# Third stage of a decoder layer in another order: each tile's factor in its own turn, low-rank products one tile sooner, the last tile's bias first

## The chip, the core and the metric

The kernel runs on one core of one Trainium2 chip. A core has five engines that run their own instruction queues side by side and wait for one another through semaphores: TensorE (PE, matmul), VectorE (DVE), ScalarE (ACT), GpSimd (POOL) and SyncE (SP, which here only issues transfers). Matmuls write to PSUM, eight banks of 128 x 512 float32; the rest lies in SBUF. The metric is the device time in microseconds. A profile is one execution with the hardware profiler on.

## The reference, cut to what matters

One decoder layer over 32 sequences of 64 tokens (2048 tokens of 512 numbers): an attention over a gathered cache, a cross attention, and a feed-forward part, each added to `x` and followed by a layer norm. Only the third part is touched:

```
z = jnp.einsum('bsd,od->bso', x, W) + b
u = jnp.einsum('bsd,edr->ebsr', x, A)
m = jnp.einsum('ebsr,ero,e->bso', u, B, p_scores)
norm_z = jnp.linalg.norm(z, axis=-1, keepdims=True)
norm_m = jnp.linalg.norm(m, axis=-1, keepdims=True)
gamma = jnp.minimum(0.5 * norm_z / (norm_m + 1e-6), 1.0)
x = _layernorm(x + z + gamma * m)
```

## The kernel before, in words

The tokens lie in 16 tiles of 128 (`NT = 16`). Three stages run one after the other, one for each part of the layer. Every product is made of three matmuls, high by high, high by low and low by high: each operand is kept as a rounded part (`...h`, made by ScalarE) and the rest (`...l`, made by VectorE or GpSimd).

The third stage is a loop over the tiles on each engine. There is no scheduler: the order of the instructions on each engine is the order in which the code is written, and the engines meet at named semaphores. For tile `tt`:

- TensorE first turns tile `tt + 5` (`turn_acc("x3", ...)`, four transposes into one of two banks of `big[0]`), then makes `z` (`linear`, 12 matmuls of 512 columns) and `m` (`low_rank_out`, three matmuls into one of three banks, `ps_mm`). Behind every fourth tile comes `low_rank(q)`, 12 matmuls that make `u` for the next four tiles. It waits for `yTl` of the last of these four (`tile_lo`), `low_rank_out` waits for `uTl` (`ff_lo`), and for the bank of three tiles back to be read (`ff_hi`, `("gm", tt - 3)`).
- VectorE makes `yTl` of tile `tt + 5` (`tile_low`, `x_lo`), adds the bias (`z_out`, matmul result plus `fbb` into `z`), works out the factor in four small steps (`mix`, steps 1 to 4, on one number per token, each waiting for the step before), makes `uTl` (`low_rank_lo`), and does the last layer norm: `measure` (two `bn_stats`, two `bn_aggr`, one addition) and `finish` (a reciprocal, and one normalise per tile). For the last three tiles, step 5 of `mix` adds `gam * m` itself. In tiles 0 and 1 it also does `normal3`, the layer norm of the second stage for tiles 12 to 15.
- ScalarE makes `yTh` (`tile_high`), the two norms and their roots (`norms`: two squares with sums, one root into `nz`), `gm_m` (`scaled_m`, the factor times `m`), `uTh` (`low_rank_hi`), and the root of the variance (`square_root`).
- GpSimd adds `z` to the tile (`add_z`), and `gm_m` (`add_m`) for all but the last three tiles. SyncE stores two tiles at a time, the last two singly.

Before the change the factor of a tile is worked out two tiles later, between the steps of `measure` and `finish`; `scaled_m` and `add_m` follow two tiles later as well.

Of the kernel before, what the change touches and what calls it, by code (L numbers as in the profile page):

```python
# [14 lines left out]
NT = T // 128  # L15
# [239 lines left out]
def decoder_kernel(nc, xt, x, ctxt, rope, wq_v, wk_v, wv_v, wo_v, k_cache, v_cache, block_idx,  # L255
                   wq2_v, bqk_in, wkv2_v, wo2_v, xbo, fw_v, fb, fa_v, fB, fp, out):
    with ExitStack() as top:
# [430 lines left out]
        def gpsimd_program(pool):  # L688
# [136 lines left out]
            def add_m(tt):  # L825
                gate.wait_ge(ff_hi, ("gm", tt))
                gate.wait_ge(pool_add, ("z", tt))
                pool.tensor_tensor(xa(tt), xa(tt), gm_m[:, tt % 2, :], ALU.add).then_inc(pool_add(("m", tt)), 1)

            for tt in range(NT):  # L830
                if 2 <= tt and tt - 2 < NT - 3:
                    add_m(tt - 2)
                add_z(tt)


# [1 line left out]
        def scalar_program(act):  # L837
# [87 lines left out]
            def square_root(tiles, tag):  # L925
                a, b = tiles[0], tiles[-1] + 1
                gate.wait_ge(ln, ("var", tag, tiles[-1]))
                act.activation(rstd[:, a:b], mv[:, a:b, 1], ACT.Sqrt).then_inc(root((tag, tiles[-1])), 1)
# [217 lines left out]
            def low_rank_hi(q):  # L1146
                gate.wait_ge(ff_done, ("u", q))
                if q >= 1:
                    gate.wait_ge(ff_done, ("m", 4 * q - 1))
                gate.wait_ge(in_pcol, "pcol")  # L1150
                act.activation(uTh[:, :], ps_u, ACT.Identity, scale=pcol[:, 0:1]).then_inc(ff_hi(("u", q)), 1)
# [13 lines left out]
            def scaled_m(tt):  # L1165
                gate.wait_ge(ff_lo, ("mix", tt, 4))
                if tt >= 2:
                    gate.wait_ge(pool_add, ("m", tt - 2))
                act.activation(gm_m[:, tt % 2, :], ps_mm[tt % 3], ACT.Copy, scale=gam[:, tt:tt + 1]).then_inc(
                    ff_hi(("gm", tt)), 1)  # L1170

            low_rank_hi(0)
            for tt in range(NT):
                if tt + 5 < NT:
                    tile_high("x3", tt + 5)
                if 2 <= tt and tt - 2 < NT - 3:
                    scaled_m(tt - 2)
                if tt >= 4 and tt % 2 == 0:
                    square_root([tt - 4, tt - 3], 3)
                norms(tt)  # L1180
                if tt < 2:
                    square_root([12 + 2 * tt, 13 + 2 * tt], 2)
                if tt % 4 == 3 and tt // 4 + 1 < 4:
                    low_rank_hi(tt // 4 + 1)
            square_root([NT - 4, NT - 3], 3)
            square_root([NT - 2], 3)
            square_root([NT - 1], 3)

        def bank_order():
# [44 lines left out]
        def vector_program(dve):  # L1234
# [365 lines left out]
            def low_rank_lo(q):  # L1600
                gate.wait_ge(ff_hi, ("u", q))
                dve.scalar_tensor_tensor(uTl[:, :], ps_u, pcol[:, 0:1], f(uTh[:, :]), ALU.mult,
                                         ALU.subtract).then_inc(ff_lo(("u", q)), 1)
# [47 lines left out]
            def finish(tiles, step):  # L1651
                if step == 0:
                    invert_root(tiles, 3, tiles[-1])
                else:
                    gate.wait_ge(ln, ("rstd", 3, tiles[-1]))
                    normalise_tile(tiles[step - 1], 3)

            low_rank_lo(0)
            for tt in range(NT):
                if tt + 5 < NT:  # L1660
                    tile_low("x3", tt + 5)
                for step in range(4):
                    if tt >= 2:
                        mix(tt - 2, step + 1)
                    if tt >= 4 and tt % 2 == 0:
                        measure([tt - 4, tt - 3], step)
                    if tt >= 5 and tt % 2 == 1 and step < 3:
                        finish([tt - 5, tt - 4], step)
                if tt >= 2:
                    mix(tt - 2, 5)  # L1670
                z_out(tt)
                if tt < 2:
                    normal3([12 + 2 * tt, 13 + 2 * tt])
                if tt % 4 == 3 and tt // 4 + 1 < 4:
                    low_rank_lo(tt // 4 + 1)
            for step in range(4):
                measure([NT - 4, NT - 3], step)
                mix(NT - 2, step + 1)
            mix(NT - 2, 5)
            for step in range(3):  # L1680
                mix(NT - 1, step + 1)
                measure([NT - 2], step)
                finish([NT - 4, NT - 3], step)
            mix(NT - 1, 4)
            mix(NT - 1, 5)
            measure([NT - 1], 0)
            finish([NT - 2], 0)
            measure([NT - 1], 1)
            finish([NT - 2], 1)
            measure([NT - 1], 2)  # L1690
            finish([NT - 1], 0)
            finish([NT - 1], 1)

        def tensor_program(pe):
# [410 lines left out]
            for tt in range(NT):  # L2107
                if tt + 5 < NT:
                    turn_acc("x3", tt + 5)
                linear(tt)  # L2110
                low_rank_out(tt)
                if tt % 4 == 3 and tt // 4 + 1 < 4:
                    low_rank(tt // 4 + 1)

        programs = (tensor_program, vector_program, scalar_program, gpsimd_program, sync_program)
# [68 lines left out]
```

## Time and profile before

| | us |
|---|---|
| median of 3 runs (2915.19 to 2920.72) | 2916.35 |
| profiled execution | 2922.1 |
| its span | 2920.3 |
| TensorE busy in the span | 2813.9 (96%) |
| VectorE busy | 1858.0 (64%) |
| ScalarE busy | 1505.8 (52%) |
| GpSimd busy | 1484.5 (51%) |

The page puts the third stage into the last of its 40 slices: of the span from 2834 to 2906 us TensorE is busy 68.63 of 72 us, VectorE 48.96; from 2906 to 2921 TensorE is busy 0.54 us, VectorE 11.38. Matmuls overlap in their rows (a matmul's row of 512 columns is 0.39 us long while the next starts after 0.23), so the time of a piece of TensorE's work is read from starts.

### The profile page before, as it was taken

The numbers are of one execution on the slowest core, as the hardware profiler recorded it, in microseconds if no ns is written. First come the engines' busy times: TensorE is split into PE (matmuls) and PEld (weight loads), VectorE is DVE, ScalarE is ACT, GpSimd is POOL, SyncE is SP. The second block draws the span as 40 slices with busy tenths as digits, with TensorE's granted clock in tenths as the row PEclk, the third lists the DMA queues.
The fourth block names the chain that finished last, engine by engine and source line by source line (L and its number), as shares of the span: only waits on it lengthen the run. The fifth ranks groups of instructions, "written<-read, shape, count | busy, mean of one in ns | idle before, by whom it ended". The sixth has DMA issues, their size and how long they took to land.

```text
span 2920.3 us, 68000 instructions
## 1 busy us (share of the span) xinstructions
PE 2813.9 (96%) x28800; PEld 2532.8 (87%) x28800; DVE 1858.0 (64%) x3294; ACT 1505.8 (52%) x3202; POOL 1484.5 (51%) x1256
## 2 busy tenths in 40 slices
PE   7999999999999999999999889999999999999997
PEld 6888888888888888888888889999999999999976
DVE  6677677677666666666666665655555566555566
ACT  5555655655565555656555544433344444343344
POOL 6777777776766666666666641212123312121124
PEclk8999999999999999999999999999999999999999
DMA  5323313313414321222222231111111111111101
GB/s 166 86 75 94 101 56 102 101 54 93 109 63 144 86 80 55 79 86 63 76 79 78 60 97 35 41 33 43 39 46 49 55 34 41 34 41 33 30 19 58
DMA packets 91500, 197.96 MB, mean 68 GB/s; under 512 B 20668, under 2 KB 21308, under 8 KB 89148
## 3 DMA queue, kind: packets, MB, share of 16 engines
q1 hardware_dynamic: 71480, 154.80, 18.6%
q10 hardware_dynamic: 17664, 34.61, 3.5%
q0 software_dynamic: 2048, 4.20, 0.6%
q8 instruction: 227, 3.72, 0.5%
q14 instruction: 81, 0.63, 0.1%
HBM read 176.78 MB, written 16.78 MB: 66 GB/s over the span
## 4 chain that ended last, share of the span: by engine, by line
PE 65%; DVE 19%; issue 6%; ACT 5%; POOL 2%; DMA 2%; ACTq 1%; SPq 0%; DVEq 0%; POOLq 0%
PE big L1708 28%; PE bank L1708 18%; PE bank L1800 11%; DVE nmx L1317 5%; PE big L1780 5%; DVE P L1323 4%; PE big L1800 3%; DVE xacc L1345 2%; DVE rall L1339 2%; DVE qTl L1312 2%; ACT qTh L849 1%; ACT P L894 1%; ACT pth L903 1%; DMA gathered<-in_k_cache,idx 1%; ACT oTh L909 1%
## 5 line engine op out<-in xcount | busy, mean ns | idle before, releaser
L729 POOL TENSOR_TENSOR ptl<-P,pth 128x576 fp32r<-128x576 f32 x512 | 725.1, 1435 | 180.8 <-ACT pth L903 179.9
L894 ACT ACTIVATE P<-big,nmx 128x576 f32<-128x576 f32 x512 | 379.3, 741 | 309.4 <-DVE nmx L1317 302.5
L1800 PE MATMUL bank<-pth,v 32*128 32x256 f32 x4608 | 432.4, 283 | 30.1 <-DVE xacc L1345 14.6
L1800 PE MATMUL big<-pth,v 32*128 32x256 f32 x4608 | 433.1, 283 | 6.4 <-issue 6.4
L1323 DVE STREAM_TRANSPOSE P<-P 128x576 f32<-128x576 f32 x512 | 386.8, 765 | 70.5 <-ACT P L894 68.2
L1800 PEld LDWEIGHTS bank<-pth,v 32*128 32x128 f32 x4608 | 391.0, 188 | 46.0 <-issue 42.6
L1317 DVE TENSOR_REDUCE nmx<-big 128x1 f32<-128x576 f32 x512 | 377.8, 749 | 6.3 <-PE big L1780 2.8
L1800 PEld LDWEIGHTS big<-pth,v 32*128 32x128 f32 x4608 | 368.4, 188 | 6.9 <-issue 6.7
L903 ACT ACTIVATE pth<-P 128x576 fp32r<-128x576 f32 x512 | 347.3, 681 | 49.2 <-DVE P L1323 48.8
L1800 PE MATMUL bank<-ptl,v 32*128 32x256 f32 x2304 | 358.1, 280 | 0.7 <-issue 0.7
L1800 PE MATMUL big<-ptl,v 32*128 32x256 f32 x2304 | 335.6, 280 | 0.0
L809 POOL TENSOR_TENSOR P<-P,sm 128x512 f32<-128x512 f32 x64 | 66.9, 1046 | 456.3 <-DVE sm L1543 456.3
L734 POOL TENSOR_TENSOR oTl<-rall,oTh 128x256 fp32r<-128x256 f32 x256 | 183.4, 738 | 210.1 <-ACT oTh L909 210.1
L1708 PE MATMUL big<-yTl,wqTh 128*128 128x256 f32 x1008 | 285.2, 283 | 0.0
L1708 PE MATMUL big<-yTh,wqTl 128*128 128x256 f32 x1008 | 285.2, 283 | 0.0
L1708 PE MATMUL big<-yTh,wqTh 128*128 128x256 f32 x1008 | 285.2, 283 | 0.0
L1466 DVE SCALAR_TENSOR_TENSOR xql<-big,bqk,xqh 128x256 fp32r<-128x256 f32 x252 | 110.1, 478 | 234.3 <-ACT xqh L1030 233.9
L909 ACT ACTIVATE oTh<-rall 128x256 fp32r<-128x256 f32 x256 | 93.5, 412 | 316.6 <-DVE rall L1339 316.6
L1800 PEld LDWEIGHTS bank<-ptl,v 32*128 32x128 f32 x2304 | 252.8, 188 | 1.5 <-issue 1.5
L1780 PE MATMUL big<-kTh,qTh 128*128 128x288 f32 x1024 | 232.6, 309 | 14.7 <-ACT P L894 12.6
L1030 ACT ACTIVATE xqh<-big,bqk 128x256 fp32r<-128x256 f32 x252 | 105.8, 471 | 252.6 <-PE big L1708 252.6
L1780 PEld LDWEIGHTS big<-kTh,qTh 128*128 128x128 f32 x1024 | 178.1, 190 | 66.6 <-issue 26.4
(277 smaller groups left out, 8367.5 us busy)
## 6 DMA issues: line engine op xcount, KB each, us to landing
rall<-kept_r ACTq DMA_DIRECT2D x64, 512.0 KB
raw<-in_wo SPq DMA_DIRECT2D x64, 256.0 KB, 2.8
raw<-in_wq SPq DMA_DIRECT2D x62, 256.0 KB, 2.8
v<-kept_v SPq DMA_DIRECT2D x24, 448.0 KB
v<-kept_v SPq DMA_DIRECT2D x68, 128.0 KB, 3.1
raw<-in_xWq SPq DMA_DIRECT2D x33, 256.0 KB, 2.7
raw<-in_xWo SPq DMA_DIRECT2D x32, 256.0 KB, 2.7
rawb<-in_xWo SPq DMA_DIRECT2D x32, 256.0 KB, 2.7
```

The lines of the kernel that those rows point to most:

```text
L729: pool.tensor_tensor(third_columns(ptl, i), blocks_of(i), f(third_columns(pth, i)), ALU.subtract).then_inc(p_low(i), 1)
L734: pool.tensor_tensor(out_quarter(ol[:, :, :], a), rall_quarter(a), f(out_quarter(oh[:, :, :], a)), ALU.subtract).then_inc(o_low((k, a)), 1)
L894: act.activation(P[:, i % PSLOTS, :].rearrange("p (k n) -> p k n", k=2), ps_s[i % 2][:, :, 0:HALF], ACT.Exp, bias=nmx[:, i % 8:i % 8 + 1], ...
L903: act.activation(third_columns(pth, i), blocks_of(i), ACT.Copy).then_inc(p_hi(i), 1)
L909: act.activation(out_quarter(oh[:, :, :], a), rall_quarter(a), ACT.Copy).then_inc(o_hi((k, a)), 1)
L1030: act.activation(q2h[:, :, p, 64 * j:64 * j + 64], ps[:, 256 * j:256 * j + 256].rearrange("p (b i) -> p b i", i=64), ACT.Identity, bias=bq ...
L1317: dve.tensor_reduce(nmx[:, i % 8:i % 8 + 1], ps_s[i % 2][:, :, 0:HALF], AX.XY, ALU.max, negate=True).then_inc(max_done(i), 1)
L1323: dve.transpose(P[:, i % PSLOTS, :], P[:, i % PSLOTS, :]).then_inc(p_turned(i), 1)
L1466: dve.scalar_tensor_tensor(q2l[:, :, p, 64 * j:64 * j + 64], ps[:, 256 * j:256 * j + 256].rearrange("p (b i) -> p b i", i=64), bqk[:, h:h ...
L1708: t = pe.matmul(dst, a, b, start=first and i == 0, stop=final and end)
L1780: m = pe.matmul(ps_s[i % 2][:, h, 0:HALF], l, r[:, HALF * h:HALF * h + HALF], start=j == 0, stop=j == 2)
L1800: m = pe.matmul(ps_o[a][:, 0:256], v[r, s, l, :], p[r, lo:hi + 1:hi - lo, block_of(b), :, :], start=first, stop=final)
```

## The change

It changes the order of the third stage, and nothing of what is computed.

- VectorE: in the turn of tile `tt` the order is now `tile_low(tt + 5)`, `z_out(tt)`, `low_rank_lo` where there is one, `measure` or `finish` of an older pair, and then all steps of `mix(tt)`. Before, `mix(tt - 2)` stood between the steps of `measure` or `finish`, ahead of `z_out(tt)`. The last tile's `z_out` now stands ahead of everything else in its turn.
- ScalarE and GpSimd: `scaled_m` and `add_m` are one tile behind the tile, not two; `low_rank_hi` stands ahead of the norms of its tile; the roots of the variance move with `measure`.
- TensorE: `low_rank` of the next four tiles is behind the third tile of four, not the fourth.

```diff
@@ gpsimd_program
             for tt in range(NT):
-                if 2 <= tt and tt - 2 < NT - 3:
-                    add_m(tt - 2)
+                if 1 <= tt and tt - 1 < NT - 3:
+                    add_m(tt - 1)
                 add_z(tt)
@@ scalar_program
                 if tt + 5 < NT:
                     tile_high("x3", tt + 5)
-                if 2 <= tt and tt - 2 < NT - 3:
-                    scaled_m(tt - 2)
-                if tt >= 4 and tt % 2 == 0:
-                    square_root([tt - 4, tt - 3], 3)
+                if 1 <= tt and tt - 1 < NT - 3:
+                    scaled_m(tt - 1)
+                if tt % 4 == 3 and tt // 4 + 1 < 4:
+                    low_rank_hi(tt // 4 + 1)
                 norms(tt)
                 if tt < 2:
                     square_root([12 + 2 * tt, 13 + 2 * tt], 2)
-                if tt % 4 == 3 and tt // 4 + 1 < 4:
-                    low_rank_hi(tt // 4 + 1)
-            square_root([NT - 4, NT - 3], 3)
-            square_root([NT - 2], 3)
+                if tt == NT - 2:
+                    square_root([NT - 4, NT - 3], 3)
+                elif tt == NT - 1:
+                    square_root([NT - 2], 3)
+                elif tt >= 3 and tt % 2 == 1:
+                    square_root([tt - 3, tt - 2], 3)
             square_root([NT - 1], 3)
@@ vector_program
                 if tt + 5 < NT:
                     tile_low("x3", tt + 5)
-                for step in range(4):
-                    if tt >= 2:
-                        mix(tt - 2, step + 1)
-                    if tt >= 4 and tt % 2 == 0:
-                        measure([tt - 4, tt - 3], step)
-                    if tt >= 5 and tt % 2 == 1 and step < 3:
-                        finish([tt - 5, tt - 4], step)
-                if tt >= 2:
-                    mix(tt - 2, 5)
                 z_out(tt)
+                if tt % 4 == 3 and tt // 4 + 1 < 4:
+                    low_rank_lo(tt // 4 + 1)
                 if tt < 2:
                     normal3([12 + 2 * tt, 13 + 2 * tt])
-                if tt % 4 == 3 and tt // 4 + 1 < 4:
-                    low_rank_lo(tt // 4 + 1)
...
+                if tt == NT - 1:
+                    for step in range(3):
+                        finish([NT - 6, NT - 5], step)
+                        measure([NT - 2], step)
+                elif tt == NT - 2:
+                    for step in range(4):
+                        measure([NT - 4, NT - 3], step)
+                elif tt >= 3 and tt % 2 == 1:
+                    for step in range(4):
+                        measure([tt - 3, tt - 2], step)
+                elif tt >= 4:
+                    for step in range(3):
+                        finish([tt - 4, tt - 3], step)
+                for step in range(5):
+                    mix(tt, step + 1)
             for step in range(3):
-                mix(NT - 1, step + 1)
-                measure([NT - 2], step)
+                measure([NT - 1], step)
                 finish([NT - 4, NT - 3], step)
...
+            for step in range(2):
+                finish([NT - 2], step)
+            for step in range(2):
+                finish([NT - 1], step)
@@ tensor_program
                 linear(tt)
                 low_rank_out(tt)
-                if tt % 4 == 3 and tt // 4 + 1 < 4:
+                if tt % 4 == 2 and tt // 4 + 1 < 4:
                     low_rank(tt // 4 + 1)
```

TensorE before, from the third tile's `m` (`bank<-wkvTh,uTh`) on: the turn of tile 8 (`ident,xaccb`), `z` and `m` of tile 3, and then the low-rank product (`bank<-yTh,xTh`), of which the first rows stand here; the rest of each product is left out.

```order
L1708 MATMUL bank<-wkvTh,uTh 128x512
...
L1701 MATMUL big<-ident,xaccb 128x128 [waits ln,tile_lo]
...
L1708 MATMUL big<-xTh,yTh 128x512 [waits ff_lo]
...
L1708 MATMUL big<-wkvTh,uTh 128x512 [waits ff_hi]
...
L1708 MATMUL bank<-yTh,xTh 128x512 [waits tile_lo]
```

The same place now:

```order
L1706 MATMUL bank<-wkvTh,uTh 128x512
...
L1706 MATMUL bank<-yTh,xTh 128x512 [waits tile_lo]
...
L1699 MATMUL big<-ident,xaccb 128x128 [waits ln]
...
L1706 MATMUL big<-xTh,yTh 128x512 [waits ff_lo]
...
L1706 MATMUL big<-wkvTh,uTh 128x512 [waits ff_hi]
```

The low-rank product has moved ahead of tile 3's products and of the turn of tile 8; its wait for tile 7's `yTl` (`tile_lo`) comes that much sooner.

VectorE before, in the turn of tile 1, behind its bias (`z`): the layer norm of tiles 14 and 15, then at once `yTl` of tile 7 and the factor of tile 0.

```order
L1611 TENSOR_TENSOR z<-big,fbb 128x512 [waits ff_done]
L1353 BN_STATS stat<-xaccb 128x6 x2
...
L1367 TENSOR_SCALAR xaccb<-xaccb,mv,rstd 128x512
L1239 TENSOR_TENSOR yTl<-big,yTh 128x4x128 [waits tile_hi]
L1617 TENSOR_SCALAR nz<-nz 128x1 [waits ff_hi]
```

Now:

```order
L1613 TENSOR_TENSOR z<-big,fbb 128x512 [waits ff_done]
L1355 BN_STATS stat<-xaccb 128x6 x2
...
L1369 TENSOR_SCALAR xaccb<-xaccb,mv,rstd 128x512
L1619 TENSOR_SCALAR nz<-nz 128x1 [waits ff_hi]
L1622 RECIPROCAL nz<-nz 128x1 [waits ff_lo]
L1625 SCALAR_TENSOR_TENSOR gam<-nz 128x1 [waits ff_lo]
L1628 TENSOR_SCALAR gam<-gam 128x1 [waits ff_lo]
L1241 TENSOR_TENSOR yTl<-big,yTh 128x4x128 [waits tile_hi]
```

The factor of tile 1 itself, with its wait for the norms (`ff_hi`), stands ahead of `yTl` of tile 7.

VectorE before, from the last bias on; the mixes of tiles 14 and 15 are the rows with `gam,xaccb`.

```order
L1611 TENSOR_TENSOR z<-big,fbb 128x512 [waits ff_done]
L1641 BN_STATS stat<-xaccb 128x6 [waits pool_add]
...
L1648 TENSOR_SCALAR mv<-mv 128x2 [waits ln]
L1626 TENSOR_SCALAR gam<-gam 128x1 [waits ff_lo]
L1630 SCALAR_TENSOR_TENSOR xaccb<-bank,gam,xaccb 128x512 [waits pool_add,ff_lo]
L1617 TENSOR_SCALAR nz<-nz 128x1 [waits ff_hi]
...
L1626 TENSOR_SCALAR gam<-gam 128x1 [waits ff_lo]
L1630 SCALAR_TENSOR_TENSOR xaccb<-big,gam,xaccb 128x512 [waits pool_add,ff_lo]
```

Now:

```order
L1613 TENSOR_TENSOR z<-big,fbb 128x512 [waits ff_done]
L1366 RECIPROCAL rstd<-rstd 128x2 [waits root]
L1643 BN_STATS stat<-xaccb 128x6 [waits acc_done]
L1369 TENSOR_SCALAR xaccb<-xaccb,mv,rstd 128x512 [waits ln]
L1647 BN_AGGR mv<-stat 128x2 [waits ln]
L1369 TENSOR_SCALAR xaccb<-xaccb,mv,rstd 128x512
L1650 TENSOR_SCALAR mv<-mv 128x1 [waits ln]
L1619 TENSOR_SCALAR nz<-nz 128x1 [waits ff_hi]
...
L1628 TENSOR_SCALAR gam<-gam 128x1 [waits ff_lo]
L1632 SCALAR_TENSOR_TENSOR xaccb<-big,gam,xaccb 128x512 [waits pool_add,ff_lo]
```

Tile 14's factor and mix have moved ahead of the last bias, and so have the statistics of tiles 12 and 13; two normalises of an older pair have moved in behind it.

## Rows read from the trace of the kernel before

**Rows 1.** Waits of TensorE, 2824 to 2921: total us, times, longest.

```profile
PE bank L1708 <- ACT gm_m L1169: 1.3, 1, 1.3
PE big L1708 <- ACT gm_m L1169: 0.8, 1, 0.8
PE bank L1708 <- DVE uTl L1602: 0.7, 1, 0.7
...
PE big L1708 <- DVE nz L1617: 0.5, 1, 0.5
```

**Rows 2.** Timeline of TensorE: start, length, engine, line, operation, tiles.

```profile
2841.69 0.60 PE L1701 MATMUL big<-ident,xacc 128*128 128x128 f32 x4
...
2845.56 0.60 PE L1701 MATMUL big<-ident,xaccb 128*128 128x128 f32 x4
...
2849.45 0.39 PE L1708 MATMUL bank<-yTh,xTh 128*128 128x512 f32 x1
...
2852.17 0.60 PE L1701 MATMUL big<-ident,xaccb 128*128 128x128 f32 x4
...
2892.03 0.39 PE L1708 MATMUL big<-xTh,yTh 128*128 128x512 f32 x1
...
2906.16 0.39 PE L1708 MATMUL big<-wkvTh,uTl 128*128 128x512 f32 x1
```

**Rows 3.** Timeline of all engines, 2909 to 2919.

```profile
2909.30 0.68 DVE L1611 TENSOR_TENSOR z<-big,fbb 128x512 f32<-128x512 f32 x1
...
2911.34 0.20 ACT L1163 ACTIVATE nz<-nrm 128x2 f32<-128x2 f32 x1
...
2914.62 0.75 DVE L1630 SCALAR_TENSOR_TENSOR xaccb<-big,gam,xaccb 128x512 f32<-128x512 f32 x1
...
2917.28 0.55 DVE L1367 TENSOR_SCALAR xaccb<-xaccb,mv,rstd 128x512 f32<-128x512 f32 x1
```

**Rows 4.** Timeline of VectorE in the first tiles of the stage.

```profile
2841.93 0.68 DVE L1239 TENSOR_TENSOR yTl<-big,yTh 128x512 fp32r<-128x512 f32 x1
2842.53 0.68 DVE L1611 TENSOR_TENSOR z<-big,fbb 128x512 f32<-128x512 f32 x1
2843.13 1.27 DVE L1353 BATCH_NORM_STATS2 stat<-xaccb 128x6 f32<-128x512 f32 x2
...
2844.72 0.17 DVE L1358 TENSOR_SCALAR mv<-mv 128x2 f32<-128x2 f32 x1
...
2846.28 0.68 DVE L1239 TENSOR_TENSOR yTl<-big,yTh 128x512 fp32r<-128x512 f32 x1
2846.88 0.14 DVE L1617 TENSOR_SCALAR nz<-nz 128x1 f32<-128x1 f32 x1
...
2847.53 0.69 DVE L1611 TENSOR_TENSOR z<-big,fbb 128x512 f32<-128x512 f32 x1
```

**Rows 5.** Timeline of all engines, 2887.7 to 2891.3.

```profile
2887.76 0.69 ACT L1169 ACTIVATE gm_m<-bank,gam 128x512 f32<-128x512 f32 x1 [2.39 <-DVE gam L1626]
...
2888.52 1.29 POOL L828 TENSOR_TENSOR xaccb<-xaccb,gm_m 128x512 f32<-128x512 f32 x1 [2.47 <-ACT gm_m L1169]
...
2888.77 1.33 DVE L1367 TENSOR_SCALAR xacc<-xacc,mv,rstd 128x512 f32<-128x512 f32 x1
...
2889.77 1.48 POOL L823 TENSOR_TENSOR xaccb<-xaccb,z 128x512 f32<-128x512 f32 x1
...
2890.02 1.25 DVE L1623 SCALAR_TENSOR_TENSOR gam<-nz 128x1 f32<-128x1 f32 x1
```

**Rows 6.** Transfers issued from 2895 to 2921: count, size, us to landing.

```profile
out<-xaccb SPq DMA_DIRECT2D x2, 256.0 KB, 2.0
```

**Rows 7.** Stretches: length, busy time by engine, granted clock, transfers.

```profile
1664.00:1668.00 4.00, 2.09 (x10) 1.40 (x8) 2.35 (x6) 0.91 (x2) 4.00 (x4) 1.00 0.61 146
1704.00:1708.00 4.00, 1.14 (x9) 0.93 (x10) 3.96 (x6) 1.95 (x4) 3.58 (x3) 1.00 0.24 67
1708.00:1712.00 4.00, 4.00 (x24) 4.00 (x23) 3.65 (x6) 0.60 (x1) 1.75 (x2) 0.57 0.90 283
```

More of the change, by code:

```diff
@@ L1661, in vector_program @@
                     tile_low("x3", tt + 5)
-                for step in range(4):
-                    if tt >= 2:
-                        mix(tt - 2, step + 1)
-                    if tt >= 4 and tt % 2 == 0:
-                        measure([tt - 4, tt - 3], step)
-                    if tt >= 5 and tt % 2 == 1 and step < 3:
-                        finish([tt - 5, tt - 4], step)
-                if tt >= 2:
-                    mix(tt - 2, 5)
                 z_out(tt)
+                if tt % 4 == 3 and tt // 4 + 1 < 4:
+                    low_rank_lo(tt // 4 + 1)
                 if tt < 2:
                     normal3([12 + 2 * tt, 13 + 2 * tt])
-                if tt % 4 == 3 and tt // 4 + 1 < 4:
-                    low_rank_lo(tt // 4 + 1)
[L1676 to L1679, printed above, removed]
+                if tt == NT - 1:
[13 more added lines that the diff above has]
+                    mix(tt, step + 1)
             for step in range(3):
-                mix(NT - 1, step + 1)
-                measure([NT - 2], step)
+                measure([NT - 1], step)
                 finish([NT - 4, NT - 3], step)
[L1684 to L1692, printed above, removed]
+            for step in range(2):
+                finish([NT - 2], step)
+            for step in range(2):
+                finish([NT - 1], step)
         def tensor_program(pe):
```

## The prediction

> **What bounds the kernel now.** I read four views, in this order: the page's busy table and slices (where the third stage lies), the waits of TensorE in that stage, the timeline of TensorE and of VectorE there, and the timeline of all engines behind the last matmul. Everything before about 2836 us of the span is untouched by the change, so only the last 85 us can move. The reader is to see three things.
>
> First, TensorE is the bound up to its last matmul, with four gaps: two in which a low-rank output product waits for `gm_m` (it needs the psum bank that ScalarE reads for `gm_m` three tiles back), one for `uTl`, and one put down to a small VectorE step, which is also the place of a `uTl` wait [rows 1]. As idle time they are 3.4 us. By starts it is a little more: a tile is 2845.56 - 2841.69 = 3.87 us of TensorE with its four transposes, a low-rank product 2852.17 - 2849.45 = 2.72 us, so a product of 512 columns starts every 0.227 us and a tile without transposes takes 15 x 0.227 = 3.40 us [rows 2]. From 2852.17 (tile 4 begins) to 2892.03 (tile 12 begins) stand 39.86 us for 7 x 3.87 + 3.40 + 2 x 2.72 = 35.93 us of work: 3.9 us lost. From there to the start of the last product at 2906.16 stand 14.13 us for 4 x 3.40 - 0.23 = 13.37: 0.7 us lost [rows 2].
>
> Second, VectorE is already behind at the end. The last bias addition (`z`, tile 15) starts at 2909.30, while the products it adds to were done about 2905.9 (0.46 before 2906.16, with a product's row of 0.39 behind its start) [rows 2, 3]: 3.4 us late.
>
> Third, from that bias the kernel needs 11.0 us to the end of the span at 2920.3: the norms (the root `nz` starts at +2.04), the last mix at 2914.62 (+5.3), the last normalise at 2917.28, done at 2917.83, and the store, 2.5 us [rows 3].
>
> **What the change removes.** (a) `gm_m` of a tile is asked for one tile earlier. A third bank back is two tile times, over 7 us, away from then on; both `gm_m` waits go. (b) The low-rank product of the next four tiles is issued behind the third tile of four, not the fourth, so `uTl` has a whole output product and 12 matmuls of cover: it still has to wait for the fourth tile's output product, which reads the old `uTh`, then costs about 0.7 on ScalarE and 0.7 on VectorE, and has 3.1 us until it is needed. Both `uTl` waits go. Sum removed: 3.9 before tile 12 and 0.7 behind it, -4.6 us if nothing takes their place.
>
> **What it adds: the wait of VectorE in its own turn.** The factor's four small steps now stand behind the bias of the same tile, and everything VectorE does for the next tile is queued behind them. The first step waits until ScalarE has the norms: 2.04 + 0.20 = 2.24 us behind the start of the bias [rows 3], of which the bias takes 0.60 (2843.13 - 2842.53) [rows 4]. Standing alone the four steps take 2847.53 - 2846.88 = 0.65 us, since each waits for the one before [rows 4]; between the statistics of another tile they are nearly hidden today.
>
> First place, the low-rank product of tiles 4 to 7, worked out in span times. VectorE now does the factor of tile 0 at 2841.93 (the end of the first late normalise), so `yTl` of tile 6 starts at 2842.58, the bias of tile 1 at 2843.18, the statistics and normalise of tiles 14 and 15 at 2843.78; these take 2846.28 - 2843.13 = 3.15, to 2846.93; the factor of tile 1 to 2847.58; and `yTl` of tile 7 is done at 2848.27 [rows 4]. TensorE wants it at the end of tile 2, at 2845.56 [rows 2]. It waits until about 2848.3, +2.8 us, where before it found it ready. The gap is new, and the change puts it there by moving the product past tile 3: +2.8 and 0.1 for a slower first matmul.
>
> Second and third place, the same product for tiles 8 to 11 and 12 to 15. Here the cover is VectorE's lag. In an odd tile VectorE does `yTl` 0.60, bias 0.60, two statistics with their short steps 2844.72 - 2843.13 + 0.1 = 1.69, factor 0.65: 3.5 us, under 3.87. In an even tile it does `yTl` 0.60, bias 0.60, a reciprocal 0.20, two normalises of 0.46 and the factor: 2.97 alone. But a normalise and the third step of the factor are held by GpSimd: beside GpSimd's two additions they took 1.33 and 1.25 us, where the same forms take about 0.5 and 0.15 otherwise; the first ended 0.29 after the addition of 2888.52 (2889.81), the second with the addition of 2889.77 (2891.25) [rows 5].
> The Trainium skill ("SBUF — State Buffer", Who interferes with whom) says the same of the cause: a VectorE operation in a two-port mode, or one with two SBUF inputs, shares one port pair with GpSimd, and whoever starts first holds it for the whole instruction; the trace agrees (1.33 and 1.25). By that rule the new order meets the lock in every even tile; without it the even tile would be 3.0 us and the rival "VectorE keeps up" below would be the forecast.
> In the new order `gm_m` follows the factor at once (0.69 long, GpSimd 0.76 behind its start [rows 5]), so GpSimd adds m of the tile before, then z, just when VectorE normalises. Followed through from tile 4 (bias at 2859.7, 1.2 late, because tile 3 also holds `uTl` behind its output product): factor of tile 4 done 2863.3, bias of tile 5 2863.9, factor of tile 5 2867.0, `yTl` of tile 11 2867.7. TensorE wants it at 2866.7: +1.1 us. Tiles 8 to 10 repeat tiles 4 to 6: again +1.1. Bounds for each of the two: 0 (VectorE not late) and 2.8 (as at the first place). I take 1.1, the chain followed row by row.
>
> Sum up to the start of tile 12: -3.9 + 2.9 + 1.1 + 1.1 and 0.2 to 0.3 of slower starts = +1.5 us, so 2893.5 for 2892.03. With the 0.7 behind it gone, TensorE ends about 0.8 later than before.
>
> **The end.** Tile 12 on, TensorE needs 3.40 per tile, VectorE more: factor and the held normalises in tile 12 (factor done 2901.4 to 2901.9), statistics of 10 and 11, factor held by the addition of z, and the mix (0.67) in tile 13, statistics of 12 and 13, factor and mix in tile 14. That gives the last bias at 2909.6 to 2910.1, about 3.4 us behind its products: as late as today. Putting that bias first removes what stood ahead of it in its own tile only, not the lag that comes from tile 14's order.
> Behind it: one statistics and two normalises of tiles 10 and 11 lie in the 1.6 us in which VectorE would wait for the norms, the first of them held by the addition of z, so the factor starts 0.6 after `nz`; the mix starts at +3.6 against +5.3 today. That is the gain of 1.7 us. Then the normalises of 12, 13 and 14 stand ahead of that of 15, where today only part did: done 3.94 behind the mix's start, today 3.21 (2917.83 - 2914.62): +0.7. And the stores of 12 and 13 (one transfer), of 14 and of 15 (256 KB, 2.0 us to landing each) are now issued within 1.4 us instead of 3.3 [rows 6]; the last may queue, 0 to 1, I take 0.6.
> Last bias to end: 11.0 - 1.7 + 0.7 + 0.6 = 10.6. End of span 2920.2 to 2920.7 against 2920.3: **about +0.2 us, nothing**. The profiled execution took 2922.1 us (1.8 around its span); the median of the runs is 5.75 us lower, and I take the difference over to it: 2916.35 + 0.2, or 2916.5.
>
> **Rivals.**
> *VectorE keeps up* (faster). Normalises and additions miss each other, the waits at the second and third low-rank product are 0, and VectorE reaches tile 15 hardly late. Tile 12 starts at 2892.03 - 3.9 + 2.9 = 2891.0, the products of tile 15 are done 13.1 later at 2904.1, the bias starts at about 2904.6, and 9.6 later is 2914.2: -6.1 us, 2910.2. For it: alone, the even tile takes 3.0. Against: the lock is in the rows [rows 5], and VectorE is 3.4 us late today with less waiting in its queue.
> *VectorE falls further behind* (slower). Both later low-rank products wait as long as the first: 2 x 1.7 more; and each pair of the last tiles costs an extra held operation, some 1 us a pair: +2.1. Sum 0.2 + 3.4 + 2.1 = +5.7: 2922.1. It decides from the point where a pair of tiles costs VectorE more than the 18.2 us that TensorE has for four (4 x 3.87 + 2.72), that is over 9.1. My pairs are at 8.2 and less.
> *The clock falls* in the new gap of 2.8 us. Where TensorE was busy 1.14 of 4 us the granted clock of the next 4 us was 0.57, so mostly at the lower level, 1.2 GHz; where it was busy 2.09 of 4 us it stayed at 1.00, 2.4 GHz [rows 7]. The new gap leaves 1.2 of 4, or more if it lies across two stretches, but work of 2.7 us goes on right behind it. Price: 4 us at 0.57, some 1.7 to 3.4 us more: 2919.
> The Trainium skill ("TensorE: Matmul & The Clock Gate", HAM oscillation) warns that an idle gap brings the slow level back; the row of 1708 shows it, that of 1664 shows a gap that did not.
>
> **How the numbers follow.** Forecast, no change to speak of: 0.74. VectorE keeps up: 0.12. Falls further behind: 0.07. Clock: 0.07. A measurement of this kernel tells about 0.2%, 5.8 us, from nothing. The first rival is just beyond it, a VectorE that keeps up only in part is not, and noise may push the forecast's lower edge over it: faster 0.13. Slower by the second rival and a part of the third: 0.07. Same: 0.80. The likeliest case alone lies within 2913 to 2920 (0 or 2.8 at two places, 0 to 1 at the store); with the rivals 2911 to 2921.5.
>
> **What would show it.** No `gm_m` or `uTl` wait of TensorE; one wait for `yTl` at the first moved low-rank product, some 2.8 us, and two of about 1; normalises of 1.3 us in even tiles; last bias about 2910 and 3 us behind its products; mix 3.6 behind it. I am wrong if the two later `yTl` waits are absent, if the last bias comes by 2906, or if the granted clock leaves 1.00 before the last matmul.

## The result, and the profile after

| | before | after |
|---|---|---|
| median of 14 runs each, same chip (us) | 2918.08 | 2923.48 |
| ratio after to before, 95% interval | | 1.0017 (1.0010 to 1.0025) |
| profiled execution / its span (us) | 2922.1 / 2920.3 | 2927.96 / 2926.2 |
| transposes of tile 7 to the end of the span (us) | 78.61 | 83.28 |

The change makes the kernel slower, by 5 us (2.9 to 7.3), which is 0.17%; the forecast was no change, 2911 to 2921.5 us, and the time lies outside its range. One execution in these runs, of the kernel "steps between", took 7002.51 us and is left out of its ratio. Of the 7.0 us between the forecast of 2916.5 and the 2923.48 measured, 1.7 belong to the kernel before, whose median is 2918.08 over 14 runs where the three runs at hand gave 2916.35; the rest is what the change did beyond the forecast.

The last line of the table is the measure used below. The place at which the third stage begins shifts from one execution to the next by some us (between 2835.33 and 2844.52 in the twelve traces of this study) through stages that no kernel here touches. So stretches are counted from the start of the transposes of tile 7 [rows 2], and not spans. By it the change costs +4.67 us, close to what the medians say. Each stretch is from one execution, so small differences need care: in "last bias first" below nothing differs from the kernel before until the last tile's turn on VectorE, and yet TensorE's last product comes 0.2 us later. Over all kernels below, differences of stretches and of medians agree within 1.3 us.

Waits of TensorE after, from 2824 on (engine, tile and line, what it waited for, us in total, times, longest), which answer to [rows 1]:

```profile
PE bank L1706 <- DVE yTl L1241: 7.2, 4, 3.3
PE big L1699 <- DVE yTl L1241: 1.0, 1, 1.0
```

All waits for `gm_m` and `uTl` are gone. One wait for `yTl` is there at each low-rank product; the rest of these two rows lies ahead of the stage. The timeline of TensorE (start, length, then line, operation and tiles; idle time before it in brackets), which answers to [rows 2]:

```profile
2842.92 0.60 PE L1699 MATMUL big<-ident,xacc 128*128 128x128 f32 x4
...
2850.25 0.47 PE L1706 MATMUL bank<-yTh,xTh 128*128 128x512 f32 x1 [3.30 <-DVE yTl L1241]
...
2854.67 0.60 PE L1699 MATMUL big<-ident,xaccb 128*128 128x128 f32 x4
...
2872.03 0.47 PE L1706 MATMUL bank<-yTh,xTh 128*128 128x512 f32 x1 [1.67 <-DVE yTl L1241]
...
2892.21 0.47 PE L1706 MATMUL bank<-yTh,xTh 128*128 128x512 f32 x1 [1.68 <-DVE yTl L1241]
...
2898.45 0.39 PE L1706 MATMUL big<-xTh,yTh 128*128 128x512 f32 x1
...
2911.82 0.39 PE L1706 MATMUL big<-wkvTh,uTl 128*128 128x512 f32 x1
```

The three waits are 3.46, 1.83 and 1.85 us by starts. By starts means: from the end of the 0.23 us that a product needs to the start of the next one. The first product also takes 4.42 us (2854.67 - 2850.25), where the second takes 2.85 (to 2874.88). The stretches around it (length, busy time of TensorE, weight loads, VectorE, ScalarE, GpSimd, then the granted clock) tell why:

```profile
2846.00:2850.00 4.00, 0.95 (x5) 0.45 (x3) 3.52 (x12) 1.90 (x6) 1.36 (x2) 1.00 0.00 0
2850.00:2854.00 4.00, 3.75 (x11) 2.98 (x12) 1.33 (x6) 1.73 (x6) 2.52 (x2) 0.65 0.00 0
2854.00:2858.00 4.00, 4.00 (x20) 3.21 (x19) 0.69 (x1) 1.18 (x2) 1.29 (x1) 0.92 0.00 0
```

From 2850 to 2854 the granted clock was 0.65: most of the product ran at the lower level, 1.2 GHz. Its matmuls start every 0.23 us up to 2851.29, a microsecond behind the gap, and every 0.43 us from there to 2854.28. VectorE and GpSimd at the first and the second place:

```profile
2846.07 1.29 POOL L823 TENSOR_TENSOR xacc<-xacc,z 128x512 f32<-128x512 f32 x1
...
2846.73 0.66 DVE L1360 TENSOR_SCALAR mv<-mv 128x2 f32<-128x2 f32 x1
...
2849.42 0.68 DVE L1241 TENSOR_TENSOR yTl<-big,yTh 128x512 fp32r<-128x512 f32 x1
...
2863.34 0.68 DVE L1613 TENSOR_TENSOR z<-big,fbb 128x512 f32<-128x512 f32 x1
...
2864.13 2.29 DVE L1369 TENSOR_SCALAR xacc<-xacc,mv,rstd 128x512 f32<-128x512 f32 x2
...
2867.58 0.68 DVE L1613 TENSOR_TENSOR z<-big,fbb 128x512 f32<-128x512 f32 x1
...
2869.12 1.29 POOL L823 TENSOR_TENSOR xacc<-xacc,z 128x512 f32<-128x512 f32 x1
...
2869.78 0.66 DVE L1650 TENSOR_SCALAR mv<-mv 128x2 f32<-128x2 f32 x1
...
2871.19 0.69 DVE L1241 TENSOR_TENSOR yTl<-big,yTh 128x512 fp32r<-128x512 f32 x1
```

From bias to bias VectorE needs 4.24 us in the even tile (2.29 of it two normalises beside GpSimd's additions) and then 3.61 us to `yTl` of the odd one. A small addition that took 0.17 at 2844.72 before [rows 4] took 0.66: it was held by GpSimd's addition of `z`, that is, it started at 2846.73 and ended with that addition, at 2847.4. (No wait of VectorE for a result of GpSimd is in this trace.) The end, which answers to [rows 3] and [rows 6]:

```profile
2915.37 0.68 DVE L1613 TENSOR_TENSOR z<-big,fbb 128x512 f32<-128x512 f32 x1
...
2918.94 0.75 DVE L1632 SCALAR_TENSOR_TENSOR xaccb<-big,gam,xaccb 128x512 f32<-128x512 f32 x1
...
2922.35 0.55 DVE L1369 TENSOR_SCALAR xaccb<-xaccb,mv,rstd 128x512 f32<-128x512 f32 x1
```

```profile
out<-xaccb SPq DMA_DIRECT2D x2, 256.0 KB, 2.8
```

The last bias is 3.8 us behind its products (done about 2911.53) and the mix 3.57 behind the bias; 10.83 us from the bias to the end.

### The profile page after: what moved, and what is told of

It reads as the page before. It is cut to its first block, busy times and chain, and to the rows that moved or that the text cites. A ratio compares the mean times of both kernels' runs of the same rounds, so it can differ in the third digit from the quotient of the medians.

```text
span 2926.2 us, 68008 instructions
## 1 busy us (share of the span) xinstructions
PE 2817.4 (96%) x28800; PEld 2536.0 (87%) x28800; DVE 1865.4 (64%) x3294; ACT 1505.2 (51%) x3202; POOL 1482.7 (51%) x1256
## 3 DMA queue, kind: packets, MB, share of 16 engines
q8 instruction: 227, 3.72, 0.5%
## 4 chain that ended last, share of the span: by engine, by line
PE 65%; DVE 20%; ACT 6%; issue 4%; DMA 2%; POOL 1%; ACTq 1%; SPq 0%; DVEq 0%; POOLq 0%
PE big L1706 28%; PE bank L1706 18%; PE bank L1798 11%; DVE nmx L1319 5%; PE big L1778 5%; DVE P L1325 4%; PE big L1798 3%; DVE xacc L1347 2%; DVE rall L1341 2%; DVE qTl L1314 2%; ACT qTh L849 1%; ACT P L894 1%; ACT pth L903 1%; ACT oTh L909 1%; PE bank L1699 1%
## 5 line engine op out<-in xcount | busy, mean ns | idle before, releaser
L1798 PE MATMUL bank<-pth,v 32*128 32x256 f32 x4608 | 433.2, 283 | 27.1 <-DVE xacc L1347 15.3
L1798 PEld LDWEIGHTS big<-pth,v 32*128 32x128 f32 x4608 | 368.8, 188 | 10.6 <-issue 10.4
```

The lines of the kernel that those rows point to most:

```text
L1798: m = pe.matmul(ps_o[a][:, 0:256], v[r, s, l, :], p[r, lo:hi + 1:hi - lo, block_of(b), :, :], start=first, stop=final)
```

## The experiments

"Stretch" is the time from the transposes of tile 7 to the end, in one profiled execution; "last product" is its part up to the start of TensorE's last product; "late" is from the end of the last tile's products to its bias; "end" from that bias on. A median difference is to runs of the kernel before on the same chip.

| kernel | ratio to before (95%) | stretch | last product | late | end |
|---|---|---|---|---|---|
| before | 1 | 78.61 | 64.47 | 3.4 | 11.0 |
| after | 1.0017 (1.0010 to 1.0025) | 83.28 | 68.90 | 3.8 | 10.8 |
| product back | 0.9981 (0.9973 to 0.9990) | 73.33 | 61.08 | 1.7 | 10.8 |
| late norm later | 1.0005 (0.9996 to 1.0014) | 79.78 | 65.40 | 3.8 | 10.8 |
| short additions | 0.9997 (0.9989 to 1.0006) | 77.28 | 66.06 | 1.3 | 10.2 |
| product only | 1.0004 (0.9995 to 1.0012) | 79.23 | 65.91 | 2.6 | 11.0 |
| bias first in each tile | 0.9982 (0.9973 to 0.9991) | 73.84 | 61.58 | 1.7 | 10.8 |
| before, bias first | 1.0011 (1.0002 to 1.0020) | 82.08 | 67.23 | 0 | 15.3 |
| last bias first | 1.0002 (0.9993 to 1.0011) | 79.49 | 64.68 | 0 | 15.1 |
| gap filled | 1.0009 (1.0000 to 1.0018) | 81.56 | 67.25 | 3.8 | 10.8 |
| factor sooner only | 1.0005 (0.9996 to 1.0013) | 80.67 | 66.61 | 4.3 | 10.0 |
| steps between | 0.9969 (0.9958 to 0.9980) | 72.75 | 60.86 | 1.4 | 10.7 |

### The product back

```diff
-                if tt % 4 == 2 and tt // 4 + 1 < 4:
+                if tt % 4 == 3 and tt // 4 + 1 < 4:
                     low_rank(tt // 4 + 1)
```

and `low_rank_hi` behind `norms`, `low_rank_lo` behind `mix` of that tile.

> The changed kernel with one part undone: TensorE's low-rank product for the next four tiles stands behind the fourth tile of four again (uTh behind the norms, uTl behind the factor of that tile). Theory A (the product asked for too soon): the three waits for yTl (3.46, 1.83 and 1.85 us by starts) go, with them the slow clock behind the first (1.6 us), and waits for uTl of 0.5 to 0.8 us each come back: 8.7 - 2.1 = 6.6 us less than the changed kernel, a little under the kernel before (2916 to 2917 beside 2918.1). Theory B (VectorE, waiting for the norms in its own turn, is too slow as such): the lag shows at the next place instead, a tile's yTl or the z bank, with 1 to 2 us per four tiles, and at most 3 us are won back: 2920 or more.

Ten us less than the changed kernel (73.33 for 83.28), and by the medians 5.5 less than the one before. TensorE keeps one wait of size, 1.0 for `uTl`. What sets this kernel apart from the one before is seen in VectorE's waits from 2848 to 2900; first before, then here:

```profile
DVE yTl L1239 <- ACT yTh L842: 12.5, 6, 2.1
DVE uTl L1602 <- ACT uTh L1151: 6.5, 3, 2.2
```

```profile
DVE nz L1619 <- ACT nz L1163: 1.6, 1, 1.6
DVE z L1613 <- PE big L1706: 1.5, 2, 0.8
```

Before, VectorE stood 2.09 us in each of six tiles, waiting for `yTh`, which ScalarE makes only after the norms of the tile before, and about as long for `uTh` in the three others. In the new order the older pair's statistics or normalises stand behind the bias and fill the time in which ScalarE makes the norms. So the new order on VectorE, ScalarE and GpSimd is worth 5 us, and the product one tile sooner loses 10 on top of it. Theory A holds, and gives more than the 6.6 it forecast: 7.8 up to the last product, and the last bias follows its products 2.1 us sooner than in the changed kernel.

### The second late layer norm one tile later

```diff
-                if tt < 2:
-                    normal3([12 + 2 * tt, 13 + 2 * tt])
+                if tt in (0, 2):
+                    normal3([12 + tt, 13 + tt])
```

> The changed kernel with the second late layer norm (tiles 14 and 15) one tile later, in the turn of tile 2 behind its bias. Theory A (the first wait comes of this norm standing ahead of yTl of tile 7, and the fall of the clock of that wait): the first wait (3.46 us) is gone, the granted clock stays at 1.00, the low-rank product takes 2.85 us rather than 4.42: 5.0 us less than the changed kernel, 2918.5, while the second and third waits stay at 1.8. Theory B (VectorE only carries the lag on): the second wait grows by 1.5 us or more and 2 us or less are won.

The first place, in TensorE's timeline:

```profile
2844.11 0.47 PE L1706 MATMUL bank<-yTh,xTh 128*128 128x512 f32 x1 [1.47 <-DVE yTl L1241]
```

The wait fell by 1.8 us only, not to nothing. VectorE's bias of tile 1 started at 2840.34, while TensorE had left tile 1 at 2838.62, so VectorE was already 1.7 us late when the moved norm would have come. That the norm of tiles 12 and 13 ahead of it made it so is read from the order; no run took that one away. The clock stayed at 1.00 and the product took 2.83. Together 3.5 us less than the changed kernel, where A said 5.0 and B 2. The other two waits stayed at 1.7, so the lag isn't carried on, as A has it. A was wrong on the size of the first wait.

### Short additions on GpSimd

```diff
-                pool.tensor_tensor(xa(tt), xa(tt), z[:, tt % 2, :], ALU.add)
+                pool.tensor_tensor(xa(tt)[:, 0:128], xa(tt)[:, 0:128], z[:, tt % 2, 0:128], ALU.add)
```

and the same for `gm_m`. The kernel leaves out three quarters of the columns of both additions, so its result is not that of the layer.

> The changed kernel, in which GpSimd's two additions of each tile work on 128 of the 512 columns (the rest of the sum is left out). Theory A (the second and third wait come of VectorE's normalises and small steps held by GpSimd's additions): the pairs of normalises take 1.0 us rather than 2.29, the second and third wait fall from 1.8 to 0.5 us or less, the first from 3.46 to about 2.9: 3.2 us less than the changed kernel, some more where the clock doesn't fall. Theory B (the lag comes of the waits for the norms alone): the two waits stay over 1.3 us, and less than 1.5 us are won.

Pairs of normalises, and the second place:

```profile
2860.12 1.17 DVE L1369 TENSOR_SCALAR xacc<-xacc,mv,rstd 128x512 f32<-128x512 f32 x2
...
2866.82 0.47 PE L1706 MATMUL bank<-yTh,xTh 128*128 128x512 f32 x1 [0.47 <-DVE yTl L1241]
```

As A has it: that GpSimd holds VectorE's instructions, called the lock from here on, makes up 1.2 us of each later wait (1.67 and 1.68 us of idle time after, 0.47 and 0.48 here). The stretch is 6.0 us shorter than after, not 3.2: 2.8 up to the last product, 2.5 in how late the last bias is and 0.6 behind it, which A had left out. The first wait stayed at 3.03 (3.30 after), and the clock fell again:

```profile
2842.00:2846.00 4.00, 1.35 (x6) 0.77 (x5) 3.52 (x13) 2.40 (x8) 0.38 (x1) 1.00 0.00 0
2846.00:2850.00 4.00, 3.63 (x9) 2.93 (x10) 1.45 (x6) 1.85 (x6) 0.91 (x2) 0.57 0.00 0
```

### The product alone in the kernel before

```diff
-                if tt % 4 == 3 and tt // 4 + 1 < 4:
+                if tt % 4 == 2 and tt // 4 + 1 < 4:
                     low_rank(tt // 4 + 1)
```

and `low_rank_hi` ahead of `norms`.

> The kernel before with one part of the change alone: the low-rank product behind the third tile of four (and uTh ahead of the norms of the fourth). Theory A: a wait for yTl of 1.4 us at the first product (VectorE ends it at 2847.0, TensorE is there at 2845.6), none at the two later ones; the waits for uTl (1.2 us together) go, those for gm_m (2.1) stay: +0.2, 2918.3. Theory B (the product one tile sooner costs as such, in clock or in a later wait for uTl): 2920 or more.

The first wait was 1.67, as A has it within 0.3. But there were two more, of 1.78 and 1.77, that it had excluded. The timeline around the second place:

```profile
2861.94 0.58 ACT L842 ACTIVATE yTh<-big 128x512 fp32r<-128x512 f32 x1
...
2862.56 0.69 DVE L1239 TENSOR_TENSOR yTl<-big,yTh 128x512 fp32r<-128x512 f32 x1 [2.09 <-ACT yTh L842]
...
2864.47 0.68 DVE L1611 TENSOR_TENSOR z<-big,fbb 128x512 f32<-128x512 f32 x1
...
2866.62 0.58 ACT L842 ACTIVATE yTh<-big 128x512 fp32r<-128x512 f32 x1
...
2868.07 0.47 PE L1708 MATMUL bank<-yTh,xTh 128*128 128x512 f32 x1 [1.78 <-DVE yTl L1239]
```

Here is what is called the loop of the old order: bias, norms, `yTh` 2.16 behind the bias, `yTl`, the older pair, the next bias, each waiting for the one before. From 2859.78 to 2864.47 it took 4.69 us. The product asked for one tile sooner meets the end of that loop, also where no late layer norm is ahead. In all +0.6 us, near A's +0.2, but by other terms: 5.2 us of waits for `yTl`, and none left for `gm_m` or `uTl`. B's later waits were there as well, of another kind than B named. So the sooner product costs 0.6 us in the old order and 10 in the new one; the two parts of the change don't add up.

### Each tile's bias ahead of yTl

```diff
+                z_out(tt)
                 if tt + 5 < NT:
                     tile_low("x3", tt + 5)
-                z_out(tt)
```

on the kernel with the product back.

> The kernel with the low-rank product back behind the fourth tile, and on VectorE each tile's bias (z) ahead of yTl of the tile five ahead. Theory A (the changed order is a loop from bias to bias: norms 2.24, factor 0.65, yTl 0.60, so 3.5 us for the 3.87 of TensorE, and VectorE cannot catch up what it is late; ahead of yTl the loop is 2.9): the bias follows its products within 0.5 us all along, the wait for uTl of 1.0 us goes, the last bias comes 1.5 us sooner behind its products: 2.5 us less than with the product back alone, 2908.7, ratio 0.9972. Theory B (VectorE's amount of work sets the last bias, not the loop): within 0.5 us of the run with the product back alone.

The bias did follow its products within 0.3 us at 2857.49 and 2861.35. Yet nothing was won: the stretch is 0.5 us longer than with the product back alone, `uTl` is still waited for (0.8) and `yTl` for 0.4, where A had the wait for `uTl` gone. The biases of the last four tiles, with the addition between two of them:

```profile
2889.09 0.69 DVE L1613 TENSOR_TENSOR z<-big,fbb 128x512 f32<-128x512 f32 x1 [0.66 <-PE big L1706]
...
2892.49 0.69 DVE L1613 TENSOR_TENSOR z<-big,fbb 128x512 f32<-128x512 f32 x1
...
2894.69 1.22 DVE L1650 TENSOR_SCALAR mv<-mv 128x2 f32<-128x2 f32 x1
...
2897.24 0.68 DVE L1613 TENSOR_TENSOR z<-big,fbb 128x512 f32<-128x512 f32 x1
2900.96 0.68 DVE L1613 TENSOR_TENSOR z<-big,fbb 128x512 f32<-128x512 f32 x1
```

VectorE was on time at tile 12 and needed 3.40, 4.75 and 3.72 us for the next three, where TensorE needs 3.40 each: it is 1.7 late again. Theory B: at the end the bound is the amount of VectorE's work in the last four tiles, held instructions among it, and not the loop.

### The kernel before with each bias first

`z_out(tt)` moved to the head of VectorE's turn in the kernel before, ahead of `tile_low`, the older factor and the older pair.

> The kernel before with one thing moved: each tile's bias stands first in VectorE's turn, ahead of yTl and of the older factor. Theory A (the old order was a loop too: bias, norms, yTh behind the norms on ScalarE, yTl, the older factor, bias, 4.7 us for the 3.87 of TensorE): VectorE's waits for yTh of 2.09 us in each tile go, so do TensorE's waits for gm_m and uTl (4.6 us), and the last bias comes up to 2.9 us sooner behind its products, of which 2 us are given back, since the factor and the mix of tile 13 now stand behind it: 5 us less than before, ratio 0.9983. Theory B (the waits for gm_m come of asking for it two tiles later): they stay or grow, 1.5 us at most are won.

Slower by 3.0 us (median) or 3.5 (stretch). Waits of TensorE:

```profile
PE big L1708 <- ACT gm_m L1169: 2.3, 4, 0.8
PE bank L1708 <- ACT gm_m L1169: 1.3, 1, 1.3
```

Theory B's picture: the factor of two tiles back now stands behind the bias, so `gm_m` is asked for later still, and its waits grow from 2.1 to 3.6 us. Theory A fails here: freeing the bias does not help while the factor follows it two tiles late.

### The last bias first, alone

```diff
+                if tt == NT - 1:
+                    z_out(tt)
                 if tt + 5 < NT:
                     tile_low("x3", tt + 5)
```

> The kernel before with the bias of the last tile alone moved to the head of its turn. Theory A (VectorE has no idle time from there to the end, so the order of its work does not matter): no change, -0.3 to +0.3 us. Theory B (the norms of the last tile are on the path): up to 1.7 us less.

Nothing won, so B is out. A's "no change" holds within the noise of the medians (+0.9 us, interval -2 to +3); the stretch is 0.9 longer, 0.2 of it ahead of anything the edit touches. In that order VectorE has no idle time behind the bias, and what stood ahead of it stands behind it: the bias is on time, and the end 15.1 us behind it rather than 11.0.

### The gap filled

```diff
+                if q == 1:
+                    for t in range(4, 7):
+                        gate.wait_ge(tile_lo, ("x3", t))
...
+                    products(ps_u[:, 0:384], fill, None, None)
                 for t in range(4 * q, 4 * q + 4):
                     gate.wait_ge(tile_lo, ("x3", t))
```

> The changed kernel; TensorE does twelve more matmuls of 384 columns (2.1 us, on tiles 4 to 6, their result overwritten) in the gap ahead of the first moved low-rank product. Theory A (the gap brings the clock down): the wait stays, as 3.5 us less 2.1, the granted clock stays at 1.00 and the product takes 2.85 us rather than 4.42: 1.6 us less than the changed kernel. Theory B (the product is slow for another reason): it takes over 4 us again and the time is the changed kernel's.

```profile
2848.38 0.50 PE L1706 MATMUL bank<-yTh,xTh 128*128 128x512 f32 x1 [1.11 <-DVE yTl L1241]
...
2851.24 0.60 PE L1699 MATMUL big<-ident,xaccb 128*128 128x128 f32 x4
```

```profile
2845.00:2849.00 4.00, 2.89 (x16) 2.48 (x15) 3.52 (x10) 1.42 (x4) 1.05 (x2) 1.00 0.00 0
2849.00:2853.00 4.00, 4.00 (x21) 3.31 (x20) 1.14 (x5) 2.58 (x7) 2.07 (x2) 1.00 0.00 0
```

The product took 2.86 us at a granted clock of 1.00, and the stretch is 1.72 shorter than after. VectorE was as late as before, so these 1.6 us were the clock's and nothing else's. That idle time ahead of work brings the slow level back is what the Trainium skill says too ("TensorE: Matmul & The Clock Gate", HAM oscillation); the traces agree for gaps of 3.0 and 3.3 us, and show 1.00 throughout behind gaps of 1.1 to 2.3. By the ratios, 1.0009 and 1.0017, the 1.6 us can't be told from noise; it is the traces that show it.

### The factor sooner, alone

```diff
-                    if tt >= 2:
-                        mix(tt - 2, step + 1)
+                    if tt >= 1:
+                        mix(tt - 1, step + 1)
```

and `scaled_m` and `add_m` of `tt - 1`, in the kernel before; the mix of tile 14 moves into the loop with it.

> The kernel before with one part of the change alone: factor, scaled m and its addition one tile behind the tile, not two; VectorE's steps still stand between those of the older pair, ahead of the bias, and the low-rank product where it was. Theory A (the old order is a loop from bias to bias, through the norms, yTh behind them on ScalarE, yTl and the older pair, 4.7 us in even tiles and 5.2 in odd ones, where TensorE needs 4.55 on the mean; its waits for gm_m only show that): the waits for gm_m (2.1 us) go, but the last bias comes no sooner: within 1 us of before, 2918. Theory B (the wait for gm_m is what costs): 3 us or more less, ratio 0.999 or lower.

Biases of tiles 4 to 6, and the waits of TensorE:

```profile
2853.10 0.69 DVE L1611 TENSOR_TENSOR z<-big,fbb 128x512 f32<-128x512 f32 x1
...
2857.79 0.68 DVE L1611 TENSOR_TENSOR z<-big,fbb 128x512 f32<-128x512 f32 x1
...
2862.96 0.69 DVE L1611 TENSOR_TENSOR z<-big,fbb 128x512 f32<-128x512 f32 x1
```

```profile
PE big L1706 <- DVE nz L1617: 2.3, 1, 2.3
PE bank L1706 <- DVE uTl L1602: 2.0, 1, 2.0
PE big L1706 <- DVE uTl L1602: 1.7, 1, 1.7
```

Theory A: no wait for `gm_m` is left, and nothing is won. The median is 0.7 us above the kernel before, and the stretch 2.1 us longer, more than the 1 us that A allowed. The loop from bias to bias still takes 4.69 and 5.17 us, and TensorE waits elsewhere, 6.0 us in all.

### Small steps between others

On the kernel with the product back, `mix(tt, 1)` between the two normalises of a pair, or between aggregation and addition of the statistics.

> The kernel with the low-rank product back behind the fourth tile, and on VectorE the first of the factor's small steps between the two normalises (or between aggregation and addition of the statistics), so that fewer of them stand alone. Theory A (a small step costs 0.19 us alone and 0.06 to 0.12 between two others, and VectorE's work sets the last bias): 0.1 us a tile in the last four, 0.3 to 0.5 us less than with the product back alone; ratio 0.998. Theory B (an order that puts a step of the factor ahead of a held operation brings GpSimd's additions sooner onto VectorE): 0.5 us or more slower than that.

The stretch is 0.58 us shorter than with the product back alone, 0.3 of it in how late the last bias is. That is A's size, but little above what two executions differ by. The ratio is the best of all, 0.9969, over seven runs that spread from 2903.07 to 2914.39, and its interval overlaps that of the product back (to 0.9980, from 0.9973). So that it beats the kernel before is shown, and that it beats the other version isn't.

## Why the prediction was wrong

**What is removed: right, for a reason that isn't the whole.** The `gm_m` and `uTl` waits went, and behind tile 12 TensorE needed 13.37 us for the 13.37 forecast. But the prediction took these waits for a matter of when `gm_m` is asked for. They were how the loop of 4.7 to 5.2 us per tile came to the surface: with the factor one tile sooner alone the `gm_m` waits went and TensorE waited 6.0 us elsewhere. It was in the trace of before, as 2.09 us of VectorE's idle time per tile, and the prediction didn't price it. That didn't spoil the sum, since the later terms were followed row by row, but it hid that the new order without the sooner product is worth 5 us.

**Up to tile 12: the terms that failed.** The waits that the change adds were there, at the three places forecast, and all three were put too small; the clock's cost behind the first was put at nothing. Forecast +1.5 us, measured 55.53 - 50.34 = +5.2. In the prediction's own terms:

| | forecast | measured | difference |
|---|---|---|---|
| wait at the first low-rank product | 2.9 | 3.46 | +0.6 |
| second and third | 1.1 and 1.1 | 1.83 and 1.85 | +1.5 |
| clock behind the first | 0 (a rival, 0.07) | 1.6 | +1.6 |

These make 3.7, and 1.5 + 3.7 is the 5.2 found.

*First wait.* The step "these take 3.15" failed: it took the statistics' addition over at 0.17 from a row where GpSimd was idle. In the new order GpSimd's addition of `z` runs beside it, and it takes 0.66; that is 0.5 of the 0.6. The prediction had spoken of GpSimd's hold for normalises and for the factor's third step, and not for this one. The Trainium skill ("VectorE: DVE Perf Modes", Mode 2×_2P) lets an instruction use both read ports if it has a single source, all in SBUF, and an even outermost dimension (or an odd one equal in source and result). The two-number addition meets that, and was held wherever an addition of `z` over 512 columns had more than 0.3 us left. The one-number additions and reciprocals kept their 0.14 to 0.17. Being small doesn't spare an instruction, though: the factor's third step, one number per token but two operands, took 0.16 mostly and 1.25 in [rows 5].

*Second and third.* The even tile came out as forecast (factor done 3.6 us behind the bias). The odd tile was put at 3.1 from bias to factor and took 3.6, by the same addition. The rest is that tile 4's bias was 1.4 late rather than 1.2, and that the forecast's own row, 2867.7 for 2866.7, is a wait of 1.0 and not 1.1. The short additions bring both waits down from 1.7 to 0.5: the lock is shown as the cause of 1.2 us of each.

*The clock.* The rival was right in mechanism, and its price of 1.7 to 3.4 us was close to the 1.6 measured; the chance was wrong. It had two rows, one behind which the clock fell and one behind which it stayed [rows 7], and for a gap of 2.8 us nothing in them chose between the two. What was set against the fall was that work goes on right behind the gap; that didn't save it, since the slow matmuls began a microsecond into that work. Filling the gap shows that the gap of 3.30 brought the clock down. Whether one of 2.8, as forecast, would have done so no run shows: 2.27 didn't, 3.03 did. So the wait that was put too small may have decided this term too. The prediction's own sign, a granted clock below 1.00 ahead of the last matmul, came true.

**The end: right.** Last bias 3.8 late (forecast 3.4), mix +3.57 (+3.6), normalise 3.96 behind the last mix's start to its end (3.94), last bias to end 10.83 (10.6), the stores 2.8 us to landing rather than 2.0. From the last bias on the sum is off by 0.2, with its lateness by 0.6. (A slip without effect: the products' end at 2905.9 before is three starts of 0.23 ahead of 2906.16, plus 0.39, and not 0.46 ahead.)

**The rivals.** "VectorE falls further behind" gave 2922.1, the nearest to the time, but not by its mechanism: nothing extra was paid in the last tiles, and the later waits grew by 0.7 and not 1.7 each. What happened is the forecast with larger waits (2.1 us) and the clock's rival (1.6 us) on top, all true at once; the cases had been priced as if only one could be.

What stays open: how much of the 1.7 us by which the last bias is still late in the best versions is held instructions and how much is bare work. Short additions in that order weren't run. Open too is why the sooner product costs so much less in the old order than in the new one; the waits say where the time went, not what a mixed order would give.

## What to carry to other kernels

Where one engine idles a fixed time in every turn (2.09 us here), look for the loop it closes: follow one turn's result through the engines back to the same instruction and compare the loop with the bound's period, before pricing the waits that the bound shows. A product moved one turn sooner asks all its inputs one turn sooner; check the latest of them against the order on the engine that makes it. And when an instruction moves to another place, its duration is that of its new neighbours: price it from a row where the same engine runs beside it.

## What the runs showed of the hardware

- An addition over 128x2 numbers took 0.17 us alone and 0.37, 0.66 or up to 1.25 beside an addition of GpSimd over 512 columns. Additions and reciprocals over 128x1 kept their 0.14 to 0.17 beside one. The factor's third step, 128x1 with two operands, took 0.16 alone and 0.62 to 1.25 beside one in the kernel before.
- Two normalises in a row took 1.00 us alone, 1.17 beside additions of 128 columns, and mostly 2.0 to 2.35 beside those of 512 (from 1.41, where an addition was half done, to 3.08, where two fell on them).
- Idle times of TensorE of 3.03 and 3.30 us ended at 2846.37 and 2850.25; the granted clock of the 4 us from 2846 and from 2850 was 0.57 and 0.65. Behind idle times of 1.11, 1.47, 1.67, 1.78 and 2.27 us it stayed at 1.00.
